# Loop bodies of 3 and 21 steps in TensorE's scans, in the place of 21 and 9

## The chip, the cores and the metric

The kernel runs on one core of a Trainium2 chip. The metric is the time of one execution on the device in microseconds (us). Before the change the median of 3 runs is 666.97 us (666.67 to 667.74). Every engine (TensorE or PE, VectorE or DVE, ScalarE or ACT, GpSimd or POOL, SyncE or SP) runs its own list of instructions, and they wait for one another by semaphores.

## The reference

An input x of 8 images, 64 channels, 64 rows and 64 columns (f32) goes through two parts. The first part is four scans, one after the other: down over the rows, up over the rows, right over the columns, left over the columns. Each scan has its own 9-tap convolution kernel K with 64 input and 64 output channels:

```
def step(prev, cur):
    new = cur + relu(row_conv(prev, K))   # 9 taps along the row, 64 -> 64 channels
    return new, new
first = x[:, 0]
_, rest = lax.scan(step, first, x[:, 1:])     # 63 steps, each needs the row before
```

The second part is a block of linear attention on the result: group norm, a 1x1 convolution to q, k and v of 4 heads, elu + 1 on q and k, the sums k^T v and q times them, a division by q times the sum of k, a 1x1 convolution, a second group norm, and the addition of the block's input. It is not touched by the change.

## The kernel before, in words

A row lies in SBUF as 128 partitions (64 channels of the even columns and 64 of the odd ones) by 8 images by 32 column pairs. By this the nine taps become five matmuls of 128 x 128 weights (`TAP_ORDER`). The f32 product is made of three f16 ones: high part of the row by high part of the weights, the row's high part scaled down by the weights' low part, and the row's low part by the weights' high part. The 8 images are two groups of 4. So a step of a scan is 2 groups x 3 parts x 5 taps = 30 pairs of weight load and matmul on PE (line 549).

The scan is a ring. In each step and for each group, DVE takes PE's sums from PSUM, applies the relu, adds the row of the input, and writes it twice (line 840: once as f16 `high`, once as f32 `state`); then it writes the low part (line 813). ACT writes the scaled copy `high_down` (line 1222) and saves the row. PE waits for `high_ready`, `down_ready` and `low_ready` of a group before the five matmuls that need them, and adds to `conv_done` behind the last.

All engines run the four scans as hardware loops (`Fori`), each with its own body: as many steps as are written out before the engine's sequencer jumps back. The constants are `SLOTS = 3` (line 22), `BODY = 9` (line 31) and `LONG_BODY = 21` (line 32). PE has a body of 21 steps in the first scan (3 passes) and of 9 in the other three (7 passes each), by line 536. DVE has 21, 12 (written out), 21 and 9; ACT has 9, 12, 9 and 9. A row's place in PSUM and SBUF is `u % SLOTS`, so a body has to be a multiple of 3 steps that divides 63. In the first step of every pass PE also waits for `w_low_ready`.

In the first scan the rows of x come from HBM by SP's queue in blocks of 7 rows (`load_raw`, line 320), into a ring of three blocks. The first three blocks wait for nothing; each later one waits until DVE has made the last row that needed its place. Between them the weights of the other scans are loaded, and GpSimd splits these into high and low parts (`split_weights`). The second scan starts to move its rows with DMAs that turn rows into columns; the third and fourth scan load nothing. In the fourth scan DVE also takes the statistics of the first group norm (line 927), in all steps of a pass but the last and not in the first pass.

PE's code stands in memory in this order: 16 warm-up matmuls, the loop of the first scan, that of the second, 5 warm-up matmuls, the loops of the third and the fourth, and the attention.

Of the kernel before, what the change touches and what calls it, by code (L numbers as in the profile page):

```python
# [21 lines left out]
SLOTS = 3  # L22
# [8 lines left out]
BODY = 9  # L31
LONG_BODY = 21
# [34 lines left out]
def columns(d):  # L67

    off = d - HALO
    return slice(max(0, -off), J - max(0, off)), slice(max(0, off), J + min(0, off))  # L70
# [16 lines left out]
def build(nc, x, k_td, k_dt, k_lr, k_rl, gn1_w, gn1_b, w_qkv, w_out, gn2_w, gn2_b, consts, out):  # L87
    with ExitStack() as ctx:
# [433 lines left out]
        def _(pe):  # L522

            def keep_busy(n, to):

                for _ in range(n):
                    nc.tensor.matmul(to[:, :], first_rows[:, :], row_of_ones[:, :], start=True, stop=True)
# [3 lines left out]
            for k in range(4):  # L531
                if k == 2:
                    keep_busy(5, bank[2])
                rows = (1, 64, 127, 190)[k]
                pe.wait_ge(w_high_ready[k], 1)
                body = LONG_BODY if k == 0 else BODY
                with pe.Fori(0, STEPS - body + 1, body) as s:
                    for u in range(body):
                        for g in range(GROUPS):
                            pe.wait_ge(high_ready[g], s + (rows + u))  # L540
                            for part_n, (rows_16, ready, w) in enumerate(
                                    ((high, None, w_high), (high_down, down_ready, w_low), (low, low_ready, w_high))):
                                if part_n == 1 and u == g == 0:
                                    pe.wait_ge(w_low_ready[k], 1)
                                if ready is not None:
                                    pe.wait_ge(ready[g], s + (rows + u))
                                for d in TAP_ORDER:
                                    to, of = columns(d)
                                    last = nc.tensor.matmul(conv_rows[g][u % SLOTS][:, :, to], w[:, k, d, :],  # L549
                                                            rows_16[:, u % SLOTS, g * GB:(g + 1) * GB, of],  # L550
                                                            start=part_n == 0 and d == HALO,
                                                            stop=part_n == 2 and d == TAP_ORDER[-1])
                            last.then_inc(conv_done[g], 1)
# [889 lines left out]
```

## Time and profile before

| what | value |
|---|---|
| median of 3 runs | 666.97 us |
| profiled execution, first to last instruction | 664.7 us |
| mean granted clock of TensorE | 0.988 of full speed |
| PE busy | 632.9 us (95%) |
| DVE busy | 568.4 us (86%) |
| ACT busy | 428.5 us (64%) |
| POOL busy | 128.2 us (19%) |
| line 549, matmuls of the scans | x7560, 421.4 us busy |

The span is from the first to the last instruction of one execution under the profiler; the median is taken over other runs. PE stands for matmuls, PEld for weight loads, PEldq for PE's sequencer (waits, registers, branches). "Idle before <- X" is how long the engine stood before an instruction, and what released it; "issue" means that no semaphore in the profile had been missing. A queue's row gives its packets, their bytes in MB, and the share of 16 DMA engines' time in that stretch.

### The profile page before, as it was taken

The page shows a single profiled execution, that of the slowest core. Times are in us where ns is not written, and L with a number is a line of the kernel's source. Part 1 is how long each engine was busy: PE and PEld are TensorE (multiplying, and loading weights), DVE is VectorE, ACT ScalarE, POOL GpSimd, SP SyncE. Part 2 cuts the span into 40 slices and gives each one's busy share as a digit, 9 for nine tenths or more (in the row PEclk, how much of TensorE's full clock was granted, in tenths as well). Part 3 has the DMA queues.
Part 4 walks back from the last instruction along what each step waited for, and adds up shares of the span by engine and source line. Part 5 has one row for each costly group of instructions (what it writes and reads, how often), then busy time and mean ns, then how long its engine had stood idle before and what let it go on. Part 6 is the DMA issues. An engine that isn't in the chain of part 4 may idle for free.

```text
span 664.7 us, 27754 instructions
## 1 busy us (share of the span) xinstructions
PE 632.9 (95%) x10562; PEld 539.5 (81%) x10562; DVE 568.4 (86%) x1953; ACT 428.5 (64%) x1062; POOL 128.2 (19%) x112
## 2 busy tenths in 40 slices
PE   7799999999999999999999999998989999999991
PEld 5799999999999899999999999965646656655650
DVE  5689989999899888989999999989868778878784
ACT  3456666677777766666665666657666867867744
POOL 0022200000000000000000000000153666666654
PEclk9999999999999999999999999999999999999996
DMA  9999990233333100000000000000326368468546
GB/s 173 207 207 186 165 178 0 52 81 80 81 79 82 41 1 0 0 0 0 0 2 0 0 0 0 0 1 2 73 70 148 78 131 179 101 125 182 115 83 127
DMA packets 79314, 50.38 MB, mean 76 GB/s; under 512 B 44256, under 2 KB 72352, under 8 KB 79264
## 3 DMA queue, kind: packets, MB, share of 16 engines
q1 hardware_dynamic: 75936, 48.91, 36.6%
q10 hardware_dynamic: 3328, 0.82, 0.6%
q8 instruction: 30, 0.49, 0.3%
q14 instruction: 20, 0.16, 0.1%
HBM read 32.34 MB, written 9.24 MB: 63 GB/s over the span
## 4 chain that ended last, share of the span: by engine, by line
PE 49%; DVE 32%; issue 10%; ACT 3%; DMA 3%; DVEq 1%; POOL 1%; ACTq 0%; SPq 0%; POOLq 0%
PE bank L549 33%; DVE scan_rows L840 7%; DVE parts L813 7%; DVE parts L840 7%; PE bank L680 3%; DVE fin L927 2%; PE bank L630 2%; DVE rows_h L1004 2%; PE bank L616 2%; DVE stats L1045 2%; DVE kp L994 1%; PE bank L669 1%; PE bank L634 1%; PE bank L604 1%; DMA rows_h<-bounce 1%
## 5 line engine op out<-in xcount | busy, mean ns | idle before, releaser
L549 PE MATMUL bank<-parts 128*128 128x124 f16 (+2 forms) x7560 | 421.4, 219 | 7.5 <-issue 4.2
L549 PEld LDWEIGHTS bank<-parts 128*128 128x128 f16 x7560 | 415.4, 98 | 14.0 <-issue 5.7
L1222 ACT ACTIVATE parts<-parts 128x128 f16<-128x128 f16 x506 | 156.6, 310 | 150.0 <-DVE parts L840 125.1
L813 DVE TENSOR_TENSOR parts<-scan_rows,parts 128x128 f16<-128x128 f32 x506 | 148.9, 294 | 14.2
L840 DVE SCALAR_TENSOR_TENSOR parts<-bank,cols_w 128x128 f16<-128x128 f32 x378 | 109.5, 290 | 22.3 <-PE bank L549 7.1
L840 DVE SCALAR_TENSOR_TENSOR scan_rows<-bank,cols_w 128x128 f32<-128x128 f32 x378 | 105.9, 280 | 0.0
L442 POOL TENSOR_TENSOR scale<-dev,half 128x2 f32<-128x2 f32 (+1 forms) x2 | 2.1, 1036 | 401.5 <-DVE dev L952 401.5
L453 POOL TENSOR_TENSOR rows_h<-rows_h 128x512 f32<-128x512 f32 x52 | 67.9, 1339 | 47.3 <-DMA rows_h<-bounce 47.3
L994 DVE SCALAR_TENSOR_TENSOR kp<-ex,bank 128x512 f32<-128x512 f32 x64 | 40.8, 679 | 21.3 <-ACT ex L1355 20.9
L1233 ACT ACTIVATE cols_w<-scan_rows 128x256 f32 x126 | 52.5, 417 | 5.7 <-issue 0.2
L1361 ACT ACTIVATE ex<-bank,minus_one 128x512 f32<-128x512 f32 x64 | 40.6, 689 | 14.6 <-PE bank L616 14.6
L1004 DVE SCALAR_TENSOR_TENSOR rows_h<-ex,bank 128x512 f32<-128x512 f32 x64 | 41.0, 683 | 5.5 <-ACT ex L1361 4.8
L1355 ACT ACTIVATE ex<-bank,minus_one 128x512 f32<-128x512 f32 x64 | 40.6, 692 | 5.3 <-PE bank L604 5.0
L840 DVE SCALAR_TENSOR_TENSOR parts<-bank,rows_h 128x128 f16<-128x128 f32 x124 | 36.0, 290 | 5.6 <-PE bank L549 0.6
L630 PE MATMUL bank<-kp,tok 128*64 128x128 f32 x512 | 35.0, 279 | 0.2 <-DVE kp L994 0.2
L630 PEld LDWEIGHTS bank<-kp,tok 128*64 128x64 f32 x512 | 27.4, 136 | 9.3 <-issue 7.3
L840 DVE SCALAR_TENSOR_TENSOR scan_rows<-bank,rows_h 128x128 f32<-128x128 f32 x124 | 34.8, 280 | 0.0
L1249 ACT ACTIVATE cols_w<-ex 128x128 f32 (+1 forms) x84 | 34.0, 414 | 0.8 <-DMA ex<-scan_rows 0.8
L1342 ACT ACTIVATE rows_h<-bank 128x512 f32<-128x512 f32 x26 | 15.5, 597 | 24.0 <-PE bank L680 22.5
L927 DVE BATCH_NORM_STATS2 fin<-cols_w x96 | 28.7, 299 | 0.0
L590 PEld LDWEIGHTS bank<-ident,parts 128*128 128x128 f16 x256 | 14.4, 98 | 16.9 <-issue 14.9
L1233 ACT ACTIVATE rows_h<-scan_rows 128x256 f32 (+1 forms) x64 | 26.6, 416 | 2.2
(146 smaller groups left out, 591.6 us busy)
## 6 DMA issues: line engine op xcount, KB each, us to landing
rows_h<-bounce SPq DMA_DIRECT2D x52, 256.0 KB, 4.8
cols_w<-x SPq DMA_DIRECT2D x6, 896.0 KB, 12.0
ex<-scan_rows SPq DMA_DIRECT2D x84, 64.0 KB, 2.0
out<-fin SPq DMA_DIRECT2D x10, 512.0 KB, 7.3
cols_w<-x SPq DMA_DIRECT2D x12, 384.0 KB, 8.6
cols_w<-x SPq DMA_DIRECT2D x12, 256.0 KB, 6.3
cols_w<-x SPq DMA_DIRECT2D x6, 512.0 KB, 10.5
kp<-scan_rows SPq DMA_DIRECT2D x40, 64.0 KB, 1.9
```

Of the source, the lines that this page charges most:

```text
L453: nc.gpsimd.tensor_tensor(qp[:, 1 - par, u, :], qp[:, 1 - par, u, :], recip_b[:, u, :], ALU.mult).then_inc(normed, 1)
L549: last = nc.tensor.matmul(conv_rows[g][u % SLOTS][:, :, to], w[:, k, d, :], rows_16[:, u % SLOTS, g * GB:(g + 1) * GB, of], start=part_n = ...
L630: nc.tensor.matmul(acc_ps[d * C:(d + 1) * C, 0:P], tok[:, i % 2, n * P + d * C:n * P + (d + 1) * C], kp[:, (2 * i + d) % 4, n * P:(n + 1) ...
L813: nc.vector.tensor_tensor(low[:, slot, gb, :], state[:, slot, gb, :] if row is None else row[:, gb, :], high[:, slot, gb, :], ALU.subtract ...
L840: nc.vector.scalar_tensor_tensor(out=to, in0=conv[g][u % SLOTS][:, 0:GB * J].rearrange("p (b j) -> p b j", b=GB), scalar=0.0, in1=add, op0 ...
L927: nc.vector.bn_stats(stats[:, b, bass.ds(n * 2 + (g - 2), 1), :].rearrange("p o s -> p (o s)"), cols[:, bass.ds(n * -BODY + (W + first), c ...
L994: nc.vector.scalar_tensor_tensor(out=kp[:, m % 4, :], in0=ex[:, m % 2, :], scalar=1.0, in1=key_ps[m % 2][:, :], op0=ALU.min, op1=ALU.max)\
L1004: nc.vector.scalar_tensor_tensor(out=qp[:, par, u, :], in0=ex[:, 2 + u % 2, :], scalar=1.0, in1=query_ps[u % 2][:, :], op0=ALU.min, op1=AL ...
L1222: act.activation(high_down[:, slot, gb, :], high[:, slot, gb, :], ACT.Copy, scale=1.0 / LOW_SCALE).then_inc(down_ready[g], 1)
L1233: act.activation(to, state[:, slot, :, :], ACT.Copy).then_inc(saved, 1)
L1355: act.activation(ex[:, m % 2, :], key_ps[m % 2][:, :], ACT.Exp, bias=minus_one[:, :])\
L1361: act.activation(ex[:, 2 + u % 2, :], query_ps[u % 2][:, :], ACT.Exp, bias=minus_one[:, :])\
```

## The change

PE's loop over the first scan has a body of 3 steps (21 passes) and its loops over the other three scans have a body of 21 steps (3 passes each). The matmuls, their order and their waits for rows are the same; the bodies of the other engines are not touched.

```
-                body = LONG_BODY if k == 0 else BODY
+                body = SLOTS if k == 0 else LONG_BODY
                 with pe.Fori(0, STEPS - body + 1, body) as s:
                     for u in range(body):
                         for g in range(GROUPS):
```

## Rows read from the trace of the kernel before

**Rows 1.** The page's chain that ended last, share of the span by engine.

```profile
PE 49%; DVE 32%; issue 10%; ACT 3%; DMA 3%; DVEq 1%; POOL 1%; ACTq 0%; SPq 0%; POOLq 0%
```

**Rows 2.** Stretches (scans one, two, four): us, engines' busy us, clock, DMA share, GB/s.

```profile
8.47:120.82 112.35, 106.48 (x1891) 104.86 (x1890) 96.42 (x376) 64.35 (x187) 11.98 (x9) 0.98 0.86 154
120.82:226.04 105.22, 105.03 (x1899) 103.78 (x1897) 94.60 (x381) 78.40 (x251) 0.00 (x0) 1.00 0.33 78
...
332.52:437.80 105.28, 105.19 (x1885) 103.11 (x1883) 100.99 (x473) 64.82 (x189) 0.00 (x0) 1.00 0.00 0
```

**Rows 3.** Order of time, first scan, weight loads: start us, us, what, count, idle before.

```profile
9.69 10.83 PEld L549 LDWEIGHTS bank<-parts 128*128 128x128 f16 x198 [0.90 <-DVE parts L266]
22.00 6.89 PEld L549 LDWEIGHTS bank<-parts 128*128 128x128 f16 x126 [1.49 <-issue]
31.43 8.33 PEld L549 LDWEIGHTS bank<-parts 128*128 128x128 f16 x126 [2.53 <-issue]
40.36 6.05 PEld L549 LDWEIGHTS bank<-parts 128*128 128x128 f16 x110 [0.60 <-issue]
```

**Rows 4.** Two short stretches of the first scan, columns as in rows 2.

```profile
31.53:34.53 3.00, 3.00 (x31) 3.00 (x32) 1.56 (x6) 1.04 (x3) 0.00 (x0) 0.50 1.17 205
36.17:37.81 1.64, 1.64 (x34) 1.64 (x32) 1.50 (x6) 1.03 (x4) 0.00 (x0) 1.00 1.23 214
```

**Rows 5.** Instruction queue q8: whole span, 9:121, 121:226, 19.2:20.7 and 125.4:126.5 us.

```profile
q8 instruction: 30, 0.49, 0.3%
...
q8 instruction: 5, 0.08, 0.4%
...
q8 instruction: 2, 0.03, 0.1%
...
q8 instruction: 1, 0.02, 5.7%
...
q8 instruction: 1, 0.02, 6.1%
```

**Rows 6.** Line 320, loads issued at 15.5, then at 51.6 and 52.2 us.

```profile
L320 SPq DMA_DIRECT2D cols_w<-x x1: 1820/1820/1820, 15.5 to 15.5; - x1
...
DMA to landing us min/median/max: 18.7/18.7/18.7
...
L320 SPq DMA_DIRECT2D cols_w<-x x2: 595/671/747, 51.6 to 52.2; - x2
...
DMA to landing us min/median/max: 9.6/11.3/13.0
```

**Rows 7.** Order of time, DVE in the first scan.

```profile
20.36 0.29 DVE L840 SCALAR_TENSOR_TENSOR parts<-bank,cols_w 128x128 f16<-128x128 f32 x1
...
46.98 1.05 DVE L813 TENSOR_TENSOR parts<-scan_rows,parts 128x128 f16<-128x128 f32 x1
...
75.92 0.29 DVE L840 SCALAR_TENSOR_TENSOR parts<-bank,cols_w 128x128 f16<-128x128 f32 x1
```

**Rows 8.** Line 537, PE's branches (ns min/median/max); order of time, second scan's loads.

```profile
L537 PEldq COMPARE_BRANCH  x24: 76/208/242, 50.4 to 438.1; - x24
...
119.94 63.24 PEld L549 LDWEIGHTS bank<-parts 128*128 128x128 f16 x1156
```

**Rows 9.** Order of time, DVE around edges of loops, third and fourth scan.

```profile
242.16 0.29 DVE L840 SCALAR_TENSOR_TENSOR parts<-bank,cols_w 128x128 f16<-128x128 f32 x1
...
243.87 0.29 DVE L840 SCALAR_TENSOR_TENSOR parts<-bank,cols_w 128x128 f16<-128x128 f32 x1 [0.15 <-issue]
...
263.46 0.29 DVE L813 TENSOR_TENSOR parts<-scan_rows,parts 128x128 f16<-128x128 f32 x1
264.18 0.29 DVE L840 SCALAR_TENSOR_TENSOR parts<-bank,cols_w 128x128 f16<-128x128 f32 x1 [0.43 <-ACT cols_w L1233]
...
363.31 0.29 DVE L813 TENSOR_TENSOR parts<-scan_rows,parts 128x128 f16<-128x128 f32 x1
364.06 0.29 DVE L840 SCALAR_TENSOR_TENSOR parts<-bank,cols_w 128x128 f16<-128x128 f32 x1 [0.46 <-ACT cols_w L1233]
```

More of the change, by code:

```diff
@@ L535, in _ @@
                 pe.wait_ge(w_high_ready[k], 1)
-                body = LONG_BODY if k == 0 else BODY
+                body = SLOTS if k == 0 else LONG_BODY
                 with pe.Fori(0, STEPS - body + 1, body) as s:
```

## The prediction

> **What bounds the kernel now.** I read the chain of waits first, then the stretches by stage, then TensorE's order of time in the first scan. The chain is half PE and a third DVE [rows 1]: the scans are a ring, PE's 30 matmuls of a step, then DVE's row, then PE again. By stage [rows 2], PE is busy for all of 105.2 us in the second scan (63 steps, 1.67 us each with all that disturbs them); the steady step is 30 weight loads of 54.7 ns (63.24 us for 1156 of them, four taken branches among them [rows 8]), 1.64 us. The first scan takes 112.35 us for the same 63 steps: some 7 us more than the second. Only there is DMA busy (share 0.86 against 0.33).
>
> Where those 7 us lie is in PE's order of time [rows 3]. PE stands before the loads at 22.00, 31.43 and 40.36 with the releaser "issue": no semaphore had been missing. Between one stand and the next lie 126 loads each time; with 126 matmuls and one register instruction per step (four of them) these are 256 instructions. The instruction queue q8 moves packets of 16 KB (30 with 0.49 MB [rows 5]), so 256 instructions of 64 bytes are one packet, and the stands are places where the next piece of code had not come. The same queue says it [rows 5]: five packets in the whole first scan, and two in the whole second. The reader is to see two things in that. The 21-step loop is read once; with 21 x 61 = 1281 instructions it is five packets long, and its second and third pass need none, as all later passes of the 9-step loops need none. And one packet starts at 19.2 and PE goes on at 22.0, some 2.8 us later.
>
> Why late? Counted from the loop's head, the first stand is at load 23 of step 6, instruction 6 x 61 + 46 = 412. So an earlier border lay at 412 - 256 = 156, in step 2, at about 13.6 us; if crossing a border asks for the block behind the one entered, that packet waited 13.6 to 19.2, 5.6 us, behind the loads of x. In the second scan the border at 412 + 4 x 256 = 1436 lies 1436 - 1285 = 151 instructions behind its head, at 124.9, and the packet starts after 125.4 [rows 5]: 0.5 us, with DMA at a third. A block lasts 126 x 54.7 ns = 6.9 us, so PE stands if the packet starts more than 6.9 - 2.8 = 4.1 us after the crossing.
>
> The Trainium skill, "Runtime: NRT & Kernel Launch", section "Instruction fetch mechanics", says that TensorE's instruction memory is refilled in blocks of 16 KiB while the current one runs; but also that it holds two lines only and that a taken branch out of them must fetch before going on. By the second sentence each pass of a long loop would fetch again; the packets of rows 5 deny it for a loop of five blocks, and the section itself gives TensorE 128 KiB. It is the second slower rival below.
>
> **The change part by part.** (1) First scan, 3 steps a pass. The loop shrinks from 1285 to about 187 instructions, and the border at 412 now lies in the second scan. No stand for code is left in the first. They cost: 9.69 to 22.00 is 12.31 us for 198 loads, which need 10.82: 1.49. 22.00 to 31.43 is 9.43 for 126 loads, which need 6.89: 2.54. 31.43 to 40.36 is 8.93 for 126: 2.04, of which 0.60 is the stand before 40.36 [rows 3]. The other 1.44 is the clock: just after the longest stand PE was granted 0.5 (1.2 GHz), and about 30 loads took 3.00 us there against 1.64 at 1.0 (2.4 GHz) [rows 4]. Without the stands I take the drop to go too. Sum: 1.49 + 2.54 + 0.60 + 1.44 = -6.1 us. Bounds: -4.6 if the drop comes anyway, -6.1 if not.
>
> (2) What is late next. DVE's row needs x. Its step 6 (counted from 0) began at 20.36, before any stand [rows 7]; step 14 would now begin at 20.36 + 8 x 1.64 = 33.5. It needs the third block of rows, whose second half is issued at 15.5, held up by nothing but the DMA queue, and lands 18.7 us later, at 34.2 [rows 6]. So +0.7 us. Bounds: 0 (a code packet less on the queue; five go down to one) and 1.5 (a semaphore's way, a second block late). All later loads are issued when a row is made, so they move along; the tightest is issued at 52.2 at the latest and lands 13.0 us later [rows 6], 10.7 us before its row is wanted at 75.92 [rows 7]: more than the 6 us gained. DVE's waits beside GpSimd's weight splits stay, as at 46.98 (1.05 us instead of 0.29 [rows 7]).
>
> (3) 18 more taken branches in the first scan (20 for 2). A branch takes 0.21 us of PE's sequencer [rows 8]. Four of them lie in the 63.24 us of the second scan, where the loads come at their steady 54.7 ns: there the sequencer's lead hides them. Each pass also repeats the wait for `w_low_ready`, which the weights met long ago; behind it stand only the pass's own matmuls, and the same four passes hide it. What would uncover one is DVE's last low part: after it come the branch and the next step's first load, some 0.5 us. In the first scan DVE's low part of the second group starts at the same place in the step, so I take 0. Bounds 0 and 18 x 0.07 = 1.3 (below).
>
> (4) The other scans have 2 taken branches each for 6. In the second they cost nothing: 0. In the third a branch away from DVE's own shows: DVE's rows at 242.16 and 243.87 are 1.71 apart [rows 9], 0.07 over 1.64. Six of them go: -0.4; the two that stay (steps 20, 41) fall on DVE's 21-step edge, where DVE's row comes 0.72 us after its last low part (263.46 to 264.18 [rows 9]). In the fourth scan all engines branch together, and the same stretch is 0.75 (363.31 to 364.06 [rows 9]): DVE's edge covers PE's, so taking six away gains at most 0.03 each, -0.1. The two new ones at steps 20 and 41 are alone, in steps where DVE adds statistics and its low part ends later: +0.2 each by my estimate from the lead in (3), +0.4 in all (bounds 0 and 0.5). Together -0.1; bounds -0.6 and +0.5.
>
> (5) New code in three scans: five borders each for two, nine more packets. In rows 5 the two of the second scan start within about 0.5 us and cost nothing; with DMA at 0.33 there and near nothing in the last two scans, 0. Cover gone, one costs the mean stand, (1.49 + 2.54 + 0.60) / 3 = 1.54.
>
> (6) The attention code moves by some 70 instructions against the blocks: 0, bounds -0.5 and +0.5 (a third of a stand).
>
> Sum: -6.1 + 0.7 + 0 - 0.1 + 0 + 0 = -5.5 us. The profiled span of 664.7 us stands 2.3 us under the median 666.97; I keep that distance: **661.5 us**.
>
> **The rivals.** *The clock falls after all.* PE stands 0.7 us or more at step 14 for x, and the granted clock drops as before: +1.4, 662.9. For it: the drop at 31.4 came right behind a stand [rows 3, 4]. Against: after the shorter first stand (22.00) there was none at once.
>
> *The branches of the short loop show.* 18 x 0.07 to 0.20 us is 1.3 to 3.6: 662.8 to 665.1. For it: the third scan's. Against: the second's, whose phase the first shares.
>
> *Slower: the stands move.* The place is the second, third and fourth scan, at the nine new borders; the price is 9 x 1.54 = 13.9, giving 675.4. It decides when a packet starts later than 4.1 us behind its crossing. For it: that is what the first scan does. Against: DMA's share there and the two packets of the second scan.
>
> *Slower: a long loop is fetched again at each pass.* Six jumps back (two in each of three scans) at one stand each, 6 x 1.54 = 9.2: 670.7. Against: no packet after the five of the first scan, whose loop jumped back twice.
>
> *The change does not do what it says:* the stands are not of code but of the loaded DMA rings, and come in the short loop too: 667.0.
>
> **How the numbers follow.** Forecast 0.70; clock 0.11; branches 0.10; stands move 0.04; fetched again 0.02; no effect 0.03. This kernel's runs spread by about 0.1%, so 0.2% (1.3 us) is what can be told from none. Faster holds the first three: 0.91; same 0.03; slower 0.06. The range: below, no wait for x and no lone branch in the fourth scan, with (6) helping, 660.0; above, the clock rival with half a microsecond of (6) or the middle of the branches' rival, 664.0. The slow cases stay outside.
>
> **What would show it.** Right: the first scan's loads in long runs with no "issue" stand before 60 us; one q8 packet or none in it, five in each of the other three; granted clock 1.0 until the tail; a DVE wait on cols_w<-x of about 0.7 us near 33.5. The first scan is then some 107 us, and the other three within 0.5 us of before. Wrong: an "issue" stand every 126 loads in the second scan, more than 16 packets up to the end of the fourth, a step of more than 1.7 us every third step in the first scan, or a first scan still at 112 us.

## The result, and the profile after

The changed kernel takes 662.93 us (median of 6 runs, 662.55 to 665.34), the kernel before 667.72 on the same chip: 4.8 us between the medians; the ratio of the runs is 0.9936, 95% interval 0.992 to 0.9952, or 4.3 us (3.2 to 5.3). The forecast was 661.5 with a range of 660.0 to 664.0. The profiled execution has a span of 660.7 us for 664.7.

By stage (stretches of the changed kernel: the four scans and what follows, columns as in [rows 2]):

```profile
8.77:115.30 106.53, 104.87 (x1891) 103.42 (x1890) 96.34 (x376) 64.70 (x187) 11.81 (x9) 1.00 0.90 162
115.30:220.53 105.23, 105.03 (x1899) 103.78 (x1897) 94.61 (x381) 78.76 (x251) 0.00 (x0) 1.00 0.33 79
220.53:326.72 106.19, 104.95 (x1890) 103.43 (x1891) 94.74 (x380) 66.52 (x192) 0.00 (x0) 1.00 0.00 1
326.72:432.91 106.19, 105.53 (x1894) 103.61 (x1891) 101.63 (x475) 65.49 (x190) 0.00 (x0) 1.00 0.00 1
432.91:660.73 227.82, 205.27 (x2985) 121.65 (x2982) 179.00 (x335) 152.57 (x242) 114.61 (x91) 0.98 0.49 103
```

Against [rows 2] the first scan is 5.8 us shorter and the second the same. By the first weight load of each scan in both traces, the third went from 106.48 to 106.19 and the fourth from 105.74 to 106.19. The scans together gave 5.6 us. What follows them went from 226.41 to 227.82: 1.4 us were given back in a part of the program that the change does not touch.

TensorE's loads in the first scan of the changed kernel, to be held against [rows 3]:

```profile
9.97 24.33 PEld L549 LDWEIGHTS bank<-parts 128*128 128x128 f16 x445 [0.73 <-DVE parts L266]
34.51 12.37 PEld L549 LDWEIGHTS bank<-parts 128*128 128x128 f16 x220 [0.21 <-DVE parts L840]
47.34 9.88 PEld L549 LDWEIGHTS bank<-parts 128*128 128x128 f16 x180 [0.46 <-DVE parts L813]
57.87 9.85 PEld L549 LDWEIGHTS bank<-parts 128*128 128x128 f16 x180 [0.66 <-DVE parts L813]
68.17 53.90 PEld L549 LDWEIGHTS bank<-parts 128*128 128x128 f16 x983 [0.45 <-DVE parts L813]
```

No stand has the releaser "issue" any more. 445 loads run through 24.33 us, four taken branches among them, at 54.7 ns. The stand at 34.51 is the wait for x that was forecast, and the three behind it are DVE's waits beside GpSimd's weight splits, which were there before.

The wait for x on DVE, and the third block's landing (order of time; line 320 in a window around its issue):

```profile
34.16 0.29 DVE L840 SCALAR_TENSOR_TENSOR parts<-bank,cols_w 128x128 f16<-128x128 f32 x1 [0.48 <-DMA cols_w<-x]
...
L320 SPq DMA_DIRECT2D cols_w<-x x2: 1840/1841/1842, 14.1 to 16.0; - x2
...
DMA to landing us min/median/max: 15.8/16.9/18.1
```

Issued at 16.0 and 18.1 us on its way, it lands at 34.1; DVE stood 0.48 us for it.

The code queue in the first scan (9:115) and in the second (115:220.5); the third and fourth give the second row again, so five packets each ([rows 5] had five in the first and two in the others):

```profile
q8 instruction: 1, 0.02, 0.1%
...
q8 instruction: 5, 0.08, 0.3%
```

### The profile page after: what moved, and what is told of

Its sections match the earlier page's. It is cut to its first block, busy times and chain, and to the rows that moved or that the text cites. A ratio compares the mean times of both kernels' runs of the same rounds, so it can differ in the third digit from the quotient of the medians.

```text
span 660.7 us, 27772 instructions
## 1 busy us (share of the span) xinstructions
PE 631.4 (96%) x10562; PEld 538.0 (81%) x10562; DVE 568.8 (86%) x1953; ACT 430.2 (65%) x1062; POOL 128.0 (19%) x112
## 4 chain that ended last, share of the span: by engine, by line
PE 41%; DVE 33%; issue 10%; DMA 6%; ACT 3%; SPq 3%; POOL 3%; DVEq 1%; ACTq 0%; POOLq 0%
PE bank L549 27%; DVE scan_rows L840 8%; DVE parts L813 8%; DVE parts L840 7%; DMA cols_w<-x 3%; DVE fin L927 2%; PE bank L680 2%; POOL rows_h L453 2%; SPq L320 2%; PE bank L630 2%; DMA rows_h<-bounce 2%; DVE rows_h L1004 2%; PE bank L616 1%; DVE kp L994 1%; DVE stats L1045 1%
## 5 line engine op out<-in xcount | busy, mean ns | idle before, releaser
L1361 ACT ACTIVATE ex<-bank,minus_one 128x512 f32<-128x512 f32 x64 | 40.6, 691 | 15.1 <-PE bank L616 15.0
L1249 ACT ACTIVATE cols_w<-ex 128x128 f32 (+1 forms) x84 | 34.1, 415 | 0.9 <-DMA ex<-scan_rows 0.8
L680 PE MATMUL bank<-rows_h,mix 128*64 128x512 f32 x96 | 25.9, 616 | 2.4 <-POOL rows_h L453 2.2
```

The source lines that it names most:

```text
L1361: act.activation(ex[:, 2 + u % 2, :], query_ps[u % 2][:, :], ACT.Exp, bias=minus_one[:, :])\
```

## The experiments

Each is named by the bodies of TensorE's four scans. Where nothing else is said, only line 536 is another, and its new text is given. In e9 to e12 all lines of the kernel behind 526 are numbered one higher, in e7 those behind `load_raw` six. All stage times are read between the first weight loads of the scans, in one profiled execution (the fourth scan ends with its last weight load); "rest" is from the last scan's end to the end of the span, and "write 1" is the first of the 13 times that the reciprocals are written to memory in the attention, from issue to landing.

| kernel | scan 1 | 2 | 3 | 4 | rest | write 1 | ratio to before, interval |
|---|---|---|---|---|---|---|---|
| before 21, 9, 9, 9 | 112.35 | 105.22 | 106.48 | 105.74 | 226.41 | 1.57 | 1 |
| changed 3, 21, 21, 21 | 106.54 | 105.23 | 106.19 | 106.19 | 227.83 | 1.57 | 0.9936, 0.992 to 0.9952 |
| e1: 3, 9, 9, 9 | 106.58 | 105.09 | 106.48 | 105.72 | 226.76 | 2.27 | 0.9934, 0.9917 to 0.9952 |
| e2: 21, 21, 21, 21 | 112.23 | 105.23 | 106.19 | 106.04 | 228.96 | 3.09 | 1.0037, 1.0017 to 1.0056 |
| e3: 3, 9, 21, 9 | 108.09 | 105.19 | 106.17 | 105.69 | 230.55 | 3.55 | 0.9955, 0.9936 to 0.9974 |
| e4: 3, 63, 63, 63 | 107.58 | 106.31 | 106.15 | 105.74 | 230.13 | 3.14 | 0.9983, 0.997 to 0.9997 |
| e5: 9, 21, 21, 21 | 107.43 | 105.51 | 106.14 | 106.08 | 227.68 | 1.92 | one run |
| e6: 63, 21, 21, 21 | 115.76 | 105.61 | 106.16 | 106.07 | 226.28 | 1.57 | one run |
| e7: before, x left out | 106.38 | 105.42 | 106.48 | 105.75 | 228.29 | 1.56 | one run |
| e8: changed, again | 107.07 | 105.26 | 106.16 | 106.20 | 229.25 | 1.57 | 0.992, 0.9899 to 0.9942 |
| e9: changed, code moved | 106.98 | 105.59 | 106.20 | 106.04 | 226.69 | 1.57 | 0.9923, 0.9905 to 0.9941 |
| e10: before, code moved | 113.10 | 105.30 | 106.48 | 105.72 | 228.29 | 2.98 | 1.002, 1.0007 to 1.0033 |
| e11: 3, 9, 21, 9, moved | 107.27 | 105.34 | 106.15 | 105.76 | 228.65 | 1.57 | 0.9921, 0.99 to 0.9943 |
| e12: 3, 21, 21, 9, moved | 107.92 | 105.19 | 106.13 | 105.72 | 226.61 | 1.58 | 0.9902, 0.9882 to 0.9923 |

**One part of the change at a time.**

```
e1  body = (SLOTS, BODY, BODY, BODY)[k]
e2  body = (LONG_BODY, LONG_BODY, LONG_BODY, LONG_BODY)[k]
```

> Bodies 3, 9, 9, 9: only the first scan is changed. Theory (code stands: a block of code comes late only while the x loads fill the DMA queue, and each scan's time hangs on its own body): scans of 106.5, 105.2, 106.5 and 105.8 us, the first as after the change and the others as before, so 5.8 us less than before up to the end of the scans; the gain of the change is all here. Rival (the long bodies earn part of it): less than 5 us of gain. What follows the scans took 226.4 before and 227.8 after: if that hangs on where the code's block borders fall there, this kernel (its code lies 182 instructions further against the blocks, the changed one 74) has a value of its own; if it is scatter between executions, anything from 226 to 228.

> Bodies 21, 21, 21, 21: only the other three scans are changed. Theory: scans of 112.3, 105.2, 106.2 and 106.2 us; the stands of the first scan and its lower clock come back whole; +0.15 us against before up to the end of the scans, so the same time as before within what can be told. Rival (nine more blocks of code cost): 1.54 us each where they come late, +13.9 us; or (the long bodies earn part of the gain): 2 us or more faster than before.

The scans came as expected, to 0.1 us: e1 has the whole gain, e2 none of it, and nine more packets cost nothing in three scans. The totals did not: e2 is 0.4% slower than before, and its rest is 2.5 us longer. That asked for the runs with moved code below.

**Where TensorE jumps back, and long straight code.**

```
e3  body = (SLOTS, BODY, LONG_BODY, BODY)[k]
e4  body = (SLOTS, STEPS, STEPS, STEPS)[k]
```

> Bodies 3, 9, 21, 9: in the third and fourth scan TensorE jumps back at the same step as VectorE. Theory (a lone jump back of TensorE costs 0.07 us in the third scan and 0.2 to 0.3 in the fourth, one beside VectorE's own jump next to nothing): scans of 106.5, 105.2, 106.2 and 105.8 us: 0.45 less than the changed kernel, all in the fourth scan. Rival (long loops cost by their code, not by where they jump): the fourth scan as after the change, 106.2, or the third as before, 106.5.

> Bodies 3, 63, 63, 63: the last three scans without a jump back, 15 blocks of code each for 5. Theory: no block comes late at the small DMA share of these scans, so scans of 106.5, 105.2, 106.1 to 106.2 and 105.8 us, some 15 packets of q8 in each of the last three, no stand with releaser issue. Rival (each block costs a little even when it comes in time): 30 more borders than after the change show as 0.02 us or more each, +0.6 us and up; rival (stands come with straight code): 1.5 us each, +45.

e3's third and fourth scan are 106.17 and 105.69: each takes the better of the two. By itself this does not part the step of the jump from the length of the code, since the third scan has the body of the changed kernel here and the fourth that of the kernel before; e4 does, with 63 steps of straight code, no jump, and 106.15 and 105.74. So long code costs nothing in these two scans, and what counts is the step of the jump. The lone jumps of the changed kernel's fourth scan are in its order of time (weight loads):

```profile
362.24 11.52 PEld L549 LDWEIGHTS bank<-parts 128*128 128x128 f16 x210 [0.24 <-issue]
...
397.67 6.58 PEld L549 LDWEIGHTS bank<-parts 128*128 128x128 f16 x120 [0.15 <-issue]
```

These are steps 21 and 42, behind the two jumps. In e4 the third and fourth scan have 15 packets each. The second is 1.1 us longer, which I had not expected; half of it is at 147.41, before which the loads stood 0.56 us for ACT (line 1222), and ACT had stood 0.98 us for a row that is moved by DMA. The issue of the row's second move at 144.5 took 1.49 us for 0.59, while a code packet ran from 144.1 to 145.6. No load stood for code. That the packet held up the row is read from the times of this one place, and no run parts the two. Both kernels' totals again fell short of their scans, with rests above 230.

**More and less code in the first scan.**

```
e5  body = (BODY, LONG_BODY, LONG_BODY, LONG_BODY)[k]
e6  body = (STEPS, LONG_BODY, LONG_BODY, LONG_BODY)[k]
```

> Bodies 9, 21, 21, 21. The first scan's loop is 553 instructions long, so of its block borders only those at 156 and 412 lie in it. Theory (a stand at every border whose packet waits behind x): exactly one stand with releaser issue, of 1.5 us, at step 6 near 20.5 us, two q8 packets in the first scan, no lower clock, and the wait for x near 34 us mostly covered: 107.5 to 108.2 us. Rival (any loop longer than the short one stands as long as the 21-step one): 112.

> Bodies 63, 21, 21, 21: the first scan as straight code, 15 blocks, every border crossed once. Theory (a border stands while x fills the DMA queue, up to about 95 us): stands with releaser issue every 126 loads up to there, some 8 to 10 of them of 0.6 to 2.5 us, one or more stretches at a clock of 0.5, none behind 100 us; 15 packets of q8; a first scan of 118 to 130 us for 112.35. Rival (only the first thousand instructions of the program come late, as the chip starts up): a first scan of 112 us still; rival (straight code always stands): stands to the end of the scan.

e5, weight loads in order of time:

```profile
10.07 10.83 PEld L549 LDWEIGHTS bank<-parts 128*128 128x128 f16 x198 [0.93 <-DVE parts L266]
22.64 25.73 PEld L549 LDWEIGHTS bank<-parts 128*128 128x128 f16 x467 [1.74 <-issue]
48.53 10.66 PEld L549 LDWEIGHTS bank<-parts 128*128 128x128 f16 x195 [0.15 <-DVE parts L813]
```

One stand, behind the same 198 loads as in [rows 3], and none at the next two places; the code queue has two packets in this scan, of 107.43 us. e6:

```profile
23.41 7.04 PEld L549 LDWEIGHTS bank<-parts 128*128 128x128 f16 x128 [1.83 <-issue]
32.89 7.04 PEld L549 LDWEIGHTS bank<-parts 128*128 128x128 f16 x128 [2.45 <-issue]
40.46 7.26 PEld L549 LDWEIGHTS bank<-parts 128*128 128x128 f16 x132 [0.53 <-issue]
...
55.83 3.10 PEld L549 LDWEIGHTS bank<-parts 128*128 128x128 f16 x56 [0.51 <-issue]
...
65.05 2.80 PEld L549 LDWEIGHTS bank<-parts 128*128 128x128 f16 x48 [1.56 <-issue]
...
102.92 27.15 PEld L549 LDWEIGHTS bank<-parts 128*128 128x128 f16 x496 [1.89 <-issue]
```

Stands go on past the 40 us of the kernel before, so the chip's start is not the reason, and the last is at 102.92, with the last x loads. There are six where I expected eight to ten: at the other borders the packet came in time. The clock did not fall at all in this scan, which took 115.76 us: more than any kernel with a jump, as the theory has it, but under the 118 to 130 that I expected, and with a stand behind 100 us where I expected none.

**The same code without x.** To `load_raw` of the kernel before, and in DVE's steps:

```
+                if n >= 1:
+                    place = (1 + n // 8, n % 8)
+                    for half in range(2):
+                        sp.dma_start(raw[half * C:(half + 1) * C, place[0], place[1]:place[1] + 1, ...],
+                                     x[0:1, :, h0 + first:h0 + first + 1, :]...).then_inc(loaded, 16)
+                    return
-                                add = raw[:, u // RAW_ROWS, gb, 1 + r * W:1 + (r + 1) * W:2]
+                                add = raw[:, 0, gb, 1 + r * W:1 + (r + 1) * W:2]
```

> The kernel before (21, 9, 9, 9) with the x rows left out: of each block of 7 rows but the first, only one row of one image is loaded, and VectorE adds the first block's rows in every step. The same instructions for TensorE and the same code packets. Theory (the packet waits behind x): the packets start within 1 us of their borders (near 14, 21, 28, 35 us), no stand with releaser issue beside the weights' own loads, clock 1.0 up to the tail, a first scan of 105.5 to 107 us. Rival (code that is read for the first time stands whatever DMA does): 4.6 us of stands and 112 us.

e7's weight loads, and the code queue in 21:22.5 and 28.2:29.7:

```profile
10.05 22.44 PEld L555 LDWEIGHTS bank<-parts 128*128 128x128 f16 x410 [0.94 <-DVE parts L266]
33.14 10.66 PEld L555 LDWEIGHTS bank<-parts 128*128 128x128 f16 x195 [0.65 <-DVE parts L819]
44.27 1.10 PEld L555 LDWEIGHTS bank<-parts 128*128 128x128 f16 x20 [0.46 <-DVE parts L819]
45.57 8.00 PEld L555 LDWEIGHTS bank<-parts 128*128 128x128 f16 x145 [0.20 <-issue]
...
q8 instruction: 1, 0.02, 3.9%
...
q8 instruction: 1, 0.02, 4.1%
```

The packets start at 15.1, 21.2, 28.3, 36.0 and 42.5, the same five blocks are read, and no load stands at a border; what is left are the waits beside GpSimd (line 819 here) and 0.20 us behind 630 loads, where the loop jumps back for the first time (why it shows here is open). The first scan is 106.38 us for 112.35. The first packet still starts some 1.2 us after its border, with the first block of x. So new code alone does not make PE stand; code whose packet waits behind x does.

**The code behind the scans, moved.** In e9 to e12 some of the warm-up matmuls (512 columns) are written as four of 128 columns: the same work, six instructions more each.

```
+            def keep_busy(n, to, quarters=0):
+                for m in range(n):
+                    for q in ([slice(0, 512)] if m >= quarters else [slice(i * P, (i + 1) * P) for i in range(4)]):
+                        nc.tensor.matmul(to[:, q], first_rows[:, :], row_of_ones[:, q], start=True, stop=True)
e9   after:   keep_busy(5, bank[2], 5)   keep_busy(11, key_ps[0], 11)   keep_busy(14, key_ps[0], 14)
e10  before:                             keep_busy(11, key_ps[0], 11)   keep_busy(14, key_ps[0], 13)
e11  body = (SLOTS, BODY, LONG_BODY, BODY)[k];       keep_busy(11, ..., 11)   keep_busy(14, ..., 7)
e12  body = (SLOTS, LONG_BODY, LONG_BODY, BODY)[k];  keep_busy(11, ..., 11)   keep_busy(14, ..., 13)
```

> The changed kernel (3, 21, 21, 21) with 30 of its warm-up matmuls (5 ahead of the third scan, 25 ahead of the attention) written as four of 128 columns each: the same work for TensorE, 180 instructions more, so the attention's code lies 254 instead of 74 instructions (of 256) further against the code blocks than before the change, next to where it lay before. Theory (a 16 KB code packet that falls into the write of the reciprocals to memory, 1.57 us alone, holds it up, and GpSimd and TensorE behind it; where the packets fall hangs on where the block borders lie): what follows the scans takes 226.4 to 226.8 us as before, not 227.8, and the first write 1.57 us with no packet in it; the kernel 1 us or more faster than the changed one. Rival (scatter of the memory's answers): 226 to 230, whatever the borders.

> The kernel before (21, 9, 9, 9), with 24 of the warm-up matmuls ahead of the attention written as four of 128 columns: 144 instructions more ahead of the attention, which is where the code of bodies 21, 21, 21, 21 (148) and 3, 9, 21, 9 (146) put it; the scans are untouched. Theory (place of the block borders): the packet meets the first write of the reciprocals, which then takes 3 us or more for 1.57; what follows the scans takes 228.5 to 230.5 us for 226.4, and the kernel 2 to 3 us more than before. Rival (scatter): no difference from before.

> Bodies 3, 9, 21, 9 with 18 of the warm-up matmuls ahead of the attention written as four of 128 columns (108 instructions more, 254 of 256 in all). Theory: scans of 106.5 to 108, 105.2, 106.2 and 105.7 us, and 226.4 to 226.8 behind them: 6 us less than before, 1 to 2 less than the changed kernel. Rival (scatter): behind the scans 226 to 230 as bodies 3, 9, 21, 9 had 230.5, and a time of 664 to 666 us.

> The changed kernel once more, for a second profile. Theory: scans of 106.5 to 107.0, 105.2, 106.2 and 106.2 us, the first write of the reciprocals 1.57 us and packets at the second, fourth, sixth and following writes as in the first profile, 227.3 to 228.3 us behind the scans. Rival (scatter): another pattern of packets and anything from 226 to 230.

> Bodies 3, 21, 21, 9 with 24 of the warm-up matmuls ahead of the attention written as four (144 instructions, 254 of 256 in all). Theory: scans of 106.5 to 107.3, 105.2, 106.2 and 105.7 us, 226.4 to 226.8 us behind them, 1 to 1.8 us faster than the changed kernel beside it. Rival: the short warm-up matmuls let the clock fall ahead of the attention as with 18 of them, 228.5 behind the scans, and the same time as the changed kernel.

Code queue and write of the reciprocals, from issue to landing: e10's first write (473.8:476.9), the changed kernel's sixth (522.9:526.3), and e9's first (468.4:470.1):

```profile
q8 instruction: 1, 0.02, 2.1%
...
bounce<-recip SPq DMA_DIRECT2D x1, 64.0 KB, 3.0
```

```profile
q8 instruction: 1, 0.02, 2.3%
...
bounce<-recip SPq DMA_DIRECT2D x1, 64.0 KB, 3.3
```

```profile
bounce<-recip SPq DMA_DIRECT2D x1, 64.0 KB, 1.6
```

The first write, of 64 KB, takes 1.57 us where no packet meets it, and 1.9 to 3.6 in the six kernels where one does. GpSimd waits for the reciprocals to come back (line 453), and PE for GpSimd. In e10 GpSimd's first four products stood 8.15 us for them, in the kernel before 6.90:

```profile
484.19 5.94 POOL L453 TENSOR_TENSOR rows_h<-rows_h 128x512 f32<-128x512 f32 x4 [8.15 <-DMA rows_h<-bounce]
```

e10 changes only how 24 warm-up matmuls are written, and with it where the attention's code lies: its first write takes 2.98, its rest is 1.9 us longer, and the kernel is slower by 0.5 to 2.2 us (its first scan, 0.75 longer in this execution with a fourth stand of 0.63 us, before the load at 48.40, may have a part in that). I had expected 2 to 3. In e9 and e12 the code is back where it lay before: first write 1.57 and 1.58, rest 226.69 and 226.61 (226.41 before) in the profiled executions. e9's total does not bear it out: I had expected 1 us or more less than the changed kernel, and its ratio of 0.9923 is that of e8, 0.992; four of its six runs are 1.4 to 1.9 us above the profiled one. The changed kernel's second profile (e8) has packets in the same eight writes as the first, but a rest of 229.25 where I expected 227.3 to 228.3. e11 has the first write at 1.57 too, but its clock fell at 447.7 for 3.4 us, ahead of the attention's first products, and its rest is 228.65; e7, whose warm-up is unchanged, lost the clock at the same place, so the short matmuls are not shown to be the cause. Nor is e11's ratio, 0.9921, below that of e8, as I had expected.

The writes alone do not give the rests. The sum of all 13 is 28.1 to 29.2 us in the kernel before, e1, e5, e9 and e12, and 31.3 to 33.0 in the changed kernel, e8, e2, e3, e4 and e10; but e5 has a rest of 227.68 with the small sum, and e6 one of 226.28 with 30.8 and packets in eight of the writes. What parts them is one instruction of GpSimd, line 468, a small step of the second group norm behind the products of line 453, and DVE's line 985 beside it. The kernel before, then the changed one:

```profile
544.74 0.34 POOL L468 TENSOR_SCALAR shift<-dev,scale,norm 128x1 f32<-128x1 f32 x1 [0.21 <-POOL scale L461]
...
545.05 1.25 DVE L985 TENSOR_SCALAR yn<-cols_w,scale,shift 128x2048 f32 x1
```

```profile
540.00 1.44 POOL L468 TENSOR_SCALAR shift<-dev,scale,norm 128x1 f32<-128x1 f32 x1 [0.21 <-POOL scale L461]
...
540.06 1.25 DVE L985 TENSOR_SCALAR yn<-cols_w,scale,shift 128x2048 f32 x1
```

Each of the 14 traces has four such pairs. 47 of the 56 instructions of line 468 start 0.16 us or more ahead of DVE's, and take 0.33 to 0.34 us. The nine that start between 0.06 us ahead of it and 0.11 us behind take 1.36 to 1.45, and end 0.13 to 0.22 us after DVE's. ACT (line 1375) waits for the result, and the next write of the reciprocals is issued 8.3 to 8.4 us after the last one instead of 6.9 to 7.1.

Rests without such an instruction: 226.28 to 226.76 (before, e1, e6, e9, e12), and 228.29 and 228.65 where the clock fell (e7, e11). With one: 227.68 to 230.55 (e5, changed, e10, e2, e3). With two: 229.25 and 230.13 (e8, e4). e2, e3, e4 and e10, whose first write took 2.98 to 3.55 us, are the upper ones of these groups. In the changed kernel the delay starts at a code packet: its sixth write has one in it and takes 3.33 us for 2.28 before, the last copy back lands 10.75 us after that write's issue for 9.86, and line 468 starts 0.25 us later, which is enough to meet DVE. So the place of the code sets which writes meet a packet, and a late copy back costs little or some 1.4 us by whether line 468 still comes ahead of line 985. This is read from the traces; no run moved one of the two instructions.

e12 is the fastest: 662.57 beside 663.67 of the changed kernel in the same round of runs, 1.1 us, as its fourth scan (0.5 less) and its rest say; the two intervals overlap, so this is not shown by the totals alone.

## Why the prediction was right, and where it was not

*First scan, stands for code: -6.1, right.* 198 and 126 loads between the stands, gone with the short loop; one stand left in a 9-step loop, more in straight code, none without x.

*The clock: not a term of its own.* I had added 1.44 us for the granted 0.5 to 4.62 us of stands. e10, the same loop, kept the clock at 1.00 in that stretch. Its loads and a stretch from 31.50 on:

```profile
22.61 6.89 PEld L550 LDWEIGHTS bank<-parts 128*128 128x128 f16 x126 [1.75 <-issue]
32.04 6.94 PEld L550 LDWEIGHTS bank<-parts 128*128 128x128 f16 x126 [2.53 <-issue]
40.85 6.93 PEld L550 LDWEIGHTS bank<-parts 128*128 128x128 f16 x126 [1.87 <-issue]
48.40 10.02 PEld L550 LDWEIGHTS bank<-parts 128*128 128x128 f16 x179 [0.63 <-issue]
...
31.50:34.50 3.00, 2.46 (x44) 2.46 (x45) 1.99 (x8) 1.22 (x4) 0.00 (x0) 1.00 1.15 197
```

There the third stand is 1.87 instead of 0.60, and PE goes on at 40.85 for 40.36. The third packet started at 37.5 before and at 37.9 in e10: its place behind x was set, and a slow PE only came to the border later. So the sum was right because the slow stretch took the place of a stand. What the rival "the clock falls after all" would have cost is not known: the clock stayed at 1.0 in the first scan of the changed kernel, where no stand for code is left to take a slow stretch in.

*The wait for x: +0.7, came as 0.48 on DVE, 0.36 on PE.* The landing was 34.1 (34.2 forecast), and the scan started 0.3 us later. Over the eight executions with a body of 3 the first scan took 106.5 to 108.1: this wait (1.3 us on DVE in e3 and in e4) and the ones beside GpSimd are its scatter.

*18 more branches in the first scan: 0, right.* All steps with a jump that no other wait touches are 1.64 us.

*Third and fourth scan: -0.4 and +0.3, came as -0.3 and +0.45.* e3 and e4 together show both signs to be a matter of which step the jump falls on.

*New code in three scans: 0, right,* with five packets each and no stand. The Trainium skill, "Runtime: NRT & Kernel Launch", section "Instruction fetch mechanics", has two lines of instruction memory and a fetch at each jump out of them; here loops of five blocks jumped back twice in each of three scans with no packet in the second and third pass, so the measurement decides against that sentence for TensorE.

*The attention: 0, bounds -0.5 and +0.5; came as +1.4.* This is the step that failed: "The attention code moves by some 70 instructions against the blocks". The bounds were for a stand of PE, a third of one. The price was paid elsewhere: a code packet fell into the sixth write of the reciprocals, the copies behind it came back late, and GpSimd's line 468 met DVE's line 985 and took 1.44 us for 0.34; ACT waits for it. e10's rest and its total say that the place of the code can cost time (what its first scan adds to the total is not taken out); that moving it back regains the 1.4 us stands on the profiled executions of e9 and e12, and e9's total does not show it. Between the two profiled spans -5.5 became -3.9 by this term, with a start 0.3 us later and 0.1 more from the scans. There is one profile of the kernel before, so its own scatter there is not known.

## What to carry to other kernels

TensorE read the first pass of a long loop block by block here (256 instructions, 16 KB), and stood where a block had to queue behind bulk loads: keep the loop short where DMA is full, and let it be long where DMA is quiet. A code packet is also DMA traffic: moving code by some hundred instructions moved packets into or out of a small transfer on which everything waits, 0.5 to 2.2 us in e10's total, as much as many edits of this size; look at that before a small difference is credited to an edit. And follow a small delay to where it ends: 0.25 us cost 1.4 here, because it put an instruction of one engine beside a long one of another. Where engines loop over the same steps, let them jump back at the same step.

## What was not expected of the hardware

The stand at full clock and the slow stretch came to the same time, because the end was set by a packet's place in the queue. A 16 KB packet, 0.9 to 1.5 us long, made the first write of 64 KB up to 2.0 us longer than its 1.57, and beside one in e4 the issue of a row's move took 1.49 us instead of 0.59. An instruction of GpSimd on 128 x 1 numbers took 1.36 to 1.45 us instead of 0.34 when it started with one of DVE, and ended just after it; why is not shown. Writing the same warm-up columns as four times as many matmuls cost nothing that could be seen.
